# Low parts of three of the ten pieces of expert weights made on GpSimd instead of VectorE, in a gated cross-attention and mixture-of-experts kernel

## What is computed

```python
x = x + tanh(g_xattn) * attention(layernorm(x), ctx, ctx, wq, wk, wv, wo)   # keys: 64 cached + 64 new
h = layernorm(x).reshape(2048, 256)
probs = softmax(h @ gate_w.T)                    # 8 experts
top_p, top_i = top_k(probs, 2)
out_e = (silu(h @ fc1[e].T) * (h @ fc2[e].T)) @ proj[e].T     # 256 -> 176 -> 256, for each expert e
y = sum of top_p * out_e over the two chosen experts
shared = (silu(h @ sfc1.T) * (h @ sfc2.T)) @ sproj.T          # 256 -> 704 -> 256
y = y + sigmoid(h @ sgate.T) * shared
x = x + tanh(g_ffn) * y
```

## Time and profile before

| | us |
|---|---|
| median of 3 runs | 299.07 |
| lowest and highest | 297.09, 299.75 |
| the profiled execution | 299.84 |
| span of its instructions | 298.0 |

### The profile page before, as it was taken

The page is one execution under the profiler, slowest core; times in us unless marked ns, Lnnn a source line. Parts: engine busy times, 40 slices in busy tenths (PEclk is TensorE's granted clock), DMA queues, the critical chain, the costliest instruction groups (busy, mean ns, idle before and its releaser), DMA issues.

```text
span 298.0 us, 5868 instructions
## 1 busy us (share of the span) xinstructions
PE 276.6 (93%) x1785; PEld 247.8 (83%) x1785; DVE 215.6 (72%) x700; ACT 170.2 (57%) x399; POOL 130.3 (44%) x157
## 2 busy tenths in 40 slices
PE   4988899999999899999999999799999999999991
PEld 3877789789779587798788888699999999998881
DVE  6667776879869748767776767877777787763285
ACT  2766678687566347574235455366676667654230
POOL 2330831542784525445550000057777787775000
PEclk9999999999999799999999999999999999999998
DMA  7470244221135202544415654358888888856796
GB/s 212 164 244 9 71 133 152 70 74 53 47 96 221 79 34 73 187 129 142 142 62 176 218 183 143 108 105 139 132 141 135 141 133 141 119 68 70 257 354 236
DMA packets 30654, 40.18 MB, mean 135 GB/s; under 512 B 2976, under 2 KB 26656, under 8 KB 30624
## 3 DMA queue, kind: packets, MB, share of 16 engines
q1 hardware_dynamic: 22480, 29.53, 31.5%
q0 software_dynamic: 7152, 9.57, 19.5%
q10 hardware_dynamic: 992, 0.71, 0.8%
HBM read 22.68 MB, written 17.11 MB: 134 GB/s over the span
## 4 chain that ended last, share of the span: by engine, by line
PE 59%; DVE 19%; issue 8%; ACT 7%; DMA 4%; POOL 1%; SPq 0%; DVEq 0%; ACTq 0%; POOLq 0%
PE bank L424 45%; PE bank L689 7%; DVE ew_lo L1060 4%; DMA xn_all<-x_dram 3%; ACT ew_hi L807 3%; PE bank L784 3%; PE bank L740 3%; DVE xt_lo L1060 2%; DVE work L1415 2%; DVE neg_max L1108 2%; ACT sh_hi L807 1%; DMA weight_stage<-ew_dram 1%; ACT work L839 1%; DVE work L1437 1%; DVE ln_stats L1071 1%
## 5 line engine op out<-in xcount | busy, mean ns | idle before, releaser
L1608 POOL DMA_INDIRECT y_d<-work,dest_of_slot x39 | 60.5, 1552 | 57.1 <-DVE dest_of_slot L1461 55.6
L424 PE MATMUL bank<-ew_hi,xt_hi 128*128 (+2 forms) x172 | 53.8, 322 | 1.1 <-DVE xt_lo L1060 0.6
L424 PE MATMUL bank<-ew_lo,xt_hi 128*128 (+2 forms) x172 | 51.8, 301 | 0.0
L424 PE MATMUL bank<-ew_hi,xt_lo 128*128 (+1 forms) x133 | 40.5, 305 | 0.0
L1060 DVE TENSOR_TENSOR xt_lo<-bank,xt_hi 128x256 fp32r<-128x256 f32 (+2 forms) x90 | 35.6, 398 | 2.8 <-ACT xt_hi L807 1.5
L1568 POOL DMA_INDIRECT xs_d<-xn_all,slot_of_pair x32 | 33.0, 1032 | 10.1 <-issue 7.3
L424 PE MATMUL bank<-xt_hi,sw_hi 128*128 128x512 f32 x88 | 34.8, 396 | 0.2 <-issue 0.2
L807 ACT ACTIVATE xt_hi<-bank 128x256 fp32r<-128x256 f32 (+1 forms) x90 | 32.8, 409 | 3.4 <-PE bank L784 2.2
L424 PE MATMUL bank<-xt_lo,sw_hi 128*128 128x512 f32 x88 | 34.5, 392 | 0.0
L424 PE MATMUL bank<-xt_hi,sw_lo 128*128 128x512 f32 x88 | 34.3, 390 | 0.0
L1060 DVE TENSOR_TENSOR ew_lo<-bank,ew_hi 128x512 fp32r<-128x512 f32 (+1 forms) x41 | 22.7, 582 | 15.9 <-ACT ew_hi L807 13.8
(11 more groups left out here) (161 smaller groups left out, 680.9 us busy)
## 6 DMA issues: line engine op xcount, KB each, us to landing
work<-xs_d SPq DMA_DIRECT2D x39, 136.0 KB
weight_stage<-ew_dram SPq DMA_DIRECT2D x10, 486.5 KB, 3.8
ew_hi<-y_d SPq DMA_DIRECT2D x8, 512.0 KB, 7.4
y_d<-work SPq DMA_DIRECT2D x6, 512.0 KB, 3.7
work<-ctx_t_dram SPq DMA_DIRECT2D x4, 512.0 KB, 3.6
xn_all<-x_dram SPq DMA_DIRECT2D x3, 512.0 KB, 6.4
xs_d<-pad_row SPq DMA_DIRECT2D x9, 136.0 KB, 1.9
weight_stage<-sw_dram SPq DMA_DIRECT2D x3, 384.0 KB
```

Source lines behind the costliest of these rows:

```text
L424: last = nc.tensor.matmul(dst, a, b, start=(n == 0), stop=(n == len(pairs) - 1))
L1608: nc.gpsimd.indirect_dma_start(out=y2_d, out_offset=bass.IndirectOffsetOnAxis(ap=IX[:, n:n + 1], axis=0), in_=EY[:, n % 4, :], in_offset=None,
```

## The change

Pieces 5, 7 and 9 (ON_POOL) get their low parts on GpSimd, with a semaphore of their own, ew_lo2. ScalarE's part is as before. VectorE leaves them out. The load of piece n waits for ew_lo2 where piece n - 2 is one of the three, so those of pieces 7 and 9. PE waits for seven counts of ew_lo and three of ew_lo2. The three subtractions stand on GpSimd behind the last scatter of stage 2.

```diff
+ON_POOL = (5, 7, 9)
...
+        ew_lo2 = sem("ew_lo_pool")
...
+        def dve_pieces(n):
+
+            return sum(i not in ON_POOL for i in range(n + 1))
...
                 if n >= 2:
                     sp.wait_ge(ew_hi, n - 1)
-                    sp.wait_ge(ew_lo, n - 1)
+                    if n - 2 in ON_POOL:
+                        sp.wait_ge(ew_lo2, ON_POOL.index(n - 2) + 1)
+                    else:
+                        sp.wait_ge(ew_lo, dve_pieces(n - 2))
...
-                        pe.wait_ge(ew_lo, E_PIECES)
+                        pe.wait_ge(ew_lo, E_PIECES - len(ON_POOL))
+                        pe.wait_ge(ew_lo2, len(ON_POOL))
                         pe.wait_ge(v_eid, 1)
                         up(0, 0)
...
-                        if PIECE_AT[n] == (s, j):
+                        if PIECE_AT[n] == (s, j) and n not in ON_POOL:
                             expert_weights(n)
...
                 for i in range(TOP):
                     scatter(c, i)
 
+            for n in ON_POOL:
+                pool.wait_ge(ew_hi, n + 1)
+                nc.gpsimd.tensor_tensor(EW[1][:, n * E_PIECE:(n + 1) * E_PIECE], ST[:, n % 2, 0:E_PIECE],
+                                        EW[0][:, n * E_PIECE:(n + 1) * E_PIECE].bitcast(F32), ALU.subtract).then_inc(ew_lo2, 1)
+
             pool.wait_ge(d_x2, 16 * N_CH)
```

## The result

| | before | after |
|---|---|---|
| median, 22 runs each, us | 298.40 | 299.65 |
| lowest and highest | 297.09, 300.06 | 298.29, 301.78 |
| profiled execution, its span | 299.84, 298.0 | 299.96, 298.2 |

The ratio after to before is 1.0044, with a 95% interval of 1.0027 to 1.0061: 1.3 us slower (0.8 to 1.8), where 1.5 was predicted. That is within 1% and inside the forecast's range of +0.5 to +2.8, and a ratio of 1 lies outside the interval. The predicted 300.6 us started from a median of 299.07; over 22 runs the kernel before has 298.40.

What follows compares the result with a forecast made beforehand. PE bounds the kernel except at the seam, where the first expert matmul waits; 172.13 + 3T + 2 x 4.74 + 0.06 gives 188.60, the tile load 188.70: plus 1.5 us, median 300.6 us, 8-in-10 range 298.4 to 303.0.

Steps and rivals of the forecast that it cites:

- T: Duration of one 128x973 low-part subtraction on GpSimd, taken as 2.31 us, with ends of 1.17 and 2.80.
- The serial chain: Pieces 5, 7, 9 share a staging buffer, so T enters three times; each turn takes T + 4.74 us.
- Rival 3: At the staging buffers: loads landing sooner or other slack covers T, giving 0 to +0.4 us; chance 0.09.
- The last step: From the end of piece 9's low part to the first expert matmul on PE: only 0.06 us for the semaphore.
- The tile load: Tile 1's load behind load 9 on SyncE's queue delays PE, ready for the expert matmul at 188.70, plus 1.5 us.
- The covers: Late work ahead of the seam stays hidden; PE's slip at pj(2,3), 0.3 to 0.5 us, adds nothing.
- The third meeting: At the seam, VectorE's s_lo(2,5) meets GpSimd's low part of piece 9 and is held to 188.55, covered.
- Rival 1: VectorE stretches GpSimd's three subtractions to 3.48, 3.00 and 3.00 us: plus 4.0 us, slower by over 1%; chance 0.17.
- Rival 2: Freed VectorE at the seam lets PE go on earlier: minus 0.7 us, needing T below 1.56 us; chance 0.06.

Runs made afterwards that it cites:

- e4_twice5: The change with piece 5's GpSimd subtraction made twice; from piece 5's high part to the first expert matmul 20.33 us, against 17.49 in the change.
- e5_third: The change with a third staging buffer for piece 7; from piece 5's high part to the first expert matmul 16.48 us, against 17.49 in the change.
- e3_six_eight: The change with pieces 6 and 8 on GpSimd instead of 5, 7, 9; piece 5's high part to first expert matmul 15.99 us, 16.11 before.
- e1_only9: The change with only piece 9 on GpSimd; from piece 5's high part to the first expert matmul 16.50 us, against 16.11 before.
- e11_reg_hidden: The change with PE's register load moved ahead of tile 0 and 1's transposes; piece 5's high part to first expert matmul 16.80 us, 17.49 in the change.
- e12_nine_reg_hidden: The change with only piece 9 on GpSimd and PE's register load ahead of the transposes; piece 5's high part to first expert matmul 15.88 us.
- e13_three_paced: Kernel before with three staging buffers, pieces 8 and 9 a block earlier, load 9 awaiting load 8; piece 5's high part to first expert matmul 15.72 us.
- e10_probe: The change with five extra GpSimd subtractions into scratch ahead of piece 5; from piece 5's high part to the first expert matmul 17.46 us.
- e9_three_dve: Kernel before with three staging buffers and pieces 8 and 9 a block earlier; piece 5's high part to first expert matmul 16.87 us, ratio 0.9981.

## Why the prediction was right, and where its terms were off

The sign, the size (+1.5 against +1.3) and the mechanism held. That the size came so close was luck: two terms were off by 0.8 us each and cancelled. By its own steps, in us from the start of low 5 (172.13 in the prediction, 170.92 measured):

| step | predicted | measured |
|---|---|---|
| T of low 5, 7, 9 | 2.31 each | 1.90, 2.28, 1.91 |
| load 7 issued | +2.38 | +1.98 |
| low 7 starts | +7.05 | +6.73 |
| load 9 issued | +9.43 | +9.08 |
| tile 1 there, its transposes start | +14.86 | +13.86 |
| PE through pj(2,4) | +16.57 | +15.57 |
| low 9 starts, ends | +14.10, +16.41 | +13.58, +15.49 |
| end of low 9 to the matmul | 0.06 | 0.91 |
| first expert matmul | +16.47 by low 9, +16.57 by the tile load | +16.40 |

- **The serial chain.** Right, and shown from three sides: lengthened (e4_twice5, passed on one for one), cut (e5_third, 1.01 us back), and moved to the buffer with slack (e3_six_eight, no cost). One turn beyond T was priced at 4.74 and measured 177.65 - 172.82 = 4.83 and 184.50 - 179.93 = 4.57, with load 9 taking 3.4 us. Rival 3 falls with it.
- **T.** Mis-sized: the sum of the three is 6.09, not 6.93. The slope of 2.20 ns per element came from two rows of different shape, 192 in one run of addresses and 256 in two blocks of 128. That part of the step between them was due to the shape is likely, but not shown. From 192 to 973 elements in one run the slope is (1900 - 597)/781 = 1.67 ns for pieces 5 and 9, and (2280 - 597)/781 = 2.15 for piece 7, close to what was assumed. The smaller T of two of the three took 0.84 us off.
- **The last step.** "With 0.06 for the semaphore" failed: it took 0.91, because the load of the expert's number stands behind the wait. e1_only9 confirms it (0.94), and e11_reg_hidden and e12_nine_reg_hidden remove it. This put 0.85 us on, so the two errors cancel almost exactly. The row that could have warned stood in the trace before, the same load at 186.0, hidden there behind the tile's low part.
- **The tile load.** The prediction took it as an equal second chain and the later of the two. It came 1.0 us earlier than priced: 0.35 from the earlier load 9 (9.08 against 9.43), and 0.65 because tile 1's transposes began 4.78 us behind load 9 (184.78 - 180.00) instead of 5.43 (184.71 - 179.28 before). So PE was through pj(2,4) at 186.49, not at the matmul's time, and the binding chain was low 9 with the register load behind it. Nor did the agreement of the two chains make the sum firmer, as the prediction has it: both contain T, so one wrong T moves both. The tile load is not idle, though: with the register load hidden it is what binds (e11_reg_hidden, 16.80 against 16.11).
- **The covers.** VectorE's operations were held as predicted, 2.08 and 1.00 us, and PE stayed at 8.00 of 8.00 us from 174 to 182: the slip of 0.3 to 0.5 us priced there did not occur. The third meeting that was priced, s_lo(2,5), fell away but for 0.08 us.
- **Rival 1** (stretching by sharing). Refuted: low 5, with low 6 waiting beside it, took 1.90 us. The 2.28 of piece 7 has no proven cause, but sharing is not it: it took 2.29 in e5_third, where s_lo(2,3) began 0.06 us ahead of its end. The mean T was 2.03, where rival 1 needed 2.85.
- **Rival 2** (freed VectorE wins). The freed VectorE is real: s_mult(2,5) no longer waits for a low part. But T would have had to be under 1.56. e12_nine_reg_hidden and e13_three_paced came 0.2 and 0.4 us of the 0.7 below before in the yardstick; neither gain is clear of the scatter in the whole times.

## What to carry to other kernels

An operation moved to a slower, idle engine is free only if nothing on the path waits for its end. The last reader of a staging buffer is such an end, since the next load waits for it: choose the buffer whose loads have slack (here that of pieces 6 and 8), or add a buffer first. Put register loads and address arithmetic ahead of a late wait, and check that the new place is itself covered. When pricing an operation by size, take the slope from rows of the same access shape where there are any, and allow for a spread: here one shape took 1.90 and 2.28 us.

## What the runs showed of the hardware

- A VectorE subtraction with two SBUF inputs and a GpSimd one exclude each other, by turns in the order in which they asked. The one held on VectorE ends a fixed time behind the other's end: 1.03 us for 973 columns, 0.55 for 512. The GpSimd side is held too: 2.72 and 2.63 us where it had to wait. That whichever starts first keeps the other out for the whole instruction is also the rule of the Trainium skill, "SBUF — State Buffer", "SBUF: two separate sides". That the turn passes to the waiting engine even when the other issues its next operation within 0.1 us (e4_twice5, e10_probe) is seen here.
- A VectorE product of 128x512 with one input in PSUM is neither held by a GpSimd subtraction nor stretches it: 0.69 us inside low 7 in the change, and low 6 with such a product inside took 1.98, against the usual 1.90 (e3_six_eight).
- A load of a register on PE from SBUF takes 0.31 to 0.50 us, and from the end of the low part that PE waited for to the matmul it was 0.91 and 0.94 (the change, e1_only9), against 0.10 with the register load ahead of the wait (e12_nine_reg_hidden).
- A load of 486.5 KB took 3.4 to 3.6 us where the last large transfer had been issued over 3 us ahead (loads 7 and 9, before and after), 4.5 where one of the same size had been issued 1.1 us ahead (load 8 before), and up to 5.7 when another such load and four tile loads were issued within 4 us (e9_three_dve).
